# Holding later weights behind the first gathers, and quantising them after the first statistics

## The reference: what is computed

```python
def _L0_tok_ref(inputs, w0, w1):
    x = w0[inputs]
    emb = jnp.einsum('blk,kh->blh', x, w1)
...
def fp4_quant_dequant(x):
    shape = x.shape
    xb = x.reshape(shape[:-1] + (shape[-1] // BLOCK, BLOCK))
    scale = jnp.max(jnp.abs(xb), axis=-1, keepdims=True) / 6.0
    scale = jnp.maximum(scale, jnp.float32(1e-12))
    xn = xb / scale
    idx = jnp.searchsorted(_MID, jnp.abs(xn))
    q = _GRID[idx] * jnp.sign(xn) * scale
    return q.reshape(shape)
...
gate = fp4_linear(x, w_gate)
y = fp4_linear(x, w_up)
h = jax.nn.silu(gate) * y
return fp4_linear(h, w_down)
```

## Time and profile before

| | us |
|---|---|
| median of 3 runs | 788.66 (787.74 to 792.24) |
| the profiled execution, its own time | 790.58 |
| span of the profiled execution, first to last instruction | 788.8 |
| PE busy | 698.7 |
| DVE busy | 600.1 |
| ACT busy | 511.7 |
| POOL busy | 147.8 |

### The profile page before, as it was taken

One profiled execution on the slowest core, in us unless ns is written; L12 is line 12 of the kernel. 1 busy time (PEld: TensorE's weight loads), 2 busy tenths in 40 slices (PEclk: granted clock), 3 DMA queues, 4 the chain that ended last, 5 costly groups with the idle time before them and its releaser, 6 DMA issues.

```text
span 788.8 us, 9882 instructions
## 1 busy us (share of the span) xinstructions
PE 698.7 (89%) x3311; PEld 566.1 (72%) x3311; DVE 600.1 (76%) x1023; ACT 511.7 (65%) x889; POOL 147.8 (19%) x220
## 2 busy tenths in 40 slices
PE   3353699699999999999999999999999999799686
PEld 2231576589688977888688958897789778688574
DVE  0797835987788888788788778888878888863763
ACT  1267488668874887389757886588748974761221
POOL 2042230433023300421022302330131003100000
PEclk9677799899999999999999999999999999899988
DMA  5800000000010000100010001000100000000000
GB/s 133 230 27 25 3 27 0 28 1 27 1 41 14 26 3 14 41 1 27 14 34 8 28 14 27 15 28 0 35 20 1 1 14 15 1 0 14 15 0 27
DMA packets 11956, 19.34 MB, mean 25 GB/s; under 512 B 972, under 2 KB 9346, under 8 KB 11906
## 3 DMA queue, kind: packets, MB, share of 16 engines
q1 hardware_dynamic: 9302, 10.31, 4.5%
q0 software_dynamic: 2560, 8.39, 3.7%
q10 hardware_dynamic: 44, 0.01, 0.0%
HBM read 14.51 MB, written 4.19 MB: 24 GB/s over the span
## 4 chain that ended last, share of the span: by engine, by line
PE 69%; DVE 15%; ACT 7%; issue 6%; DMA 2%; POOL 0%; SPq 0%; DVEq 0%; ACTq 0%; POOLq 0%
PE psB L546 17%; PE psB L573 11%; PE psC L642 11%; PE psC L615 11%; PE psA L537 9%; PE psA L509 3%; PE psC L629 3%; ACT mix L796 2%; DMA kkT<-L_ffn_w_gate 2%; DVE top L352 1%; DVE mix L1082 1%; PE psB L519 1%; PE psA L519 1%; DVE top L949 1%; ACT take L790 1%
## 5 line engine op out<-in xcount | busy, mean ns | idle before, releaser
L546 PE MATMUL psB<-cwv_s,kkT 128*128 128x256 f32 x512 | 113.2, 379 | 0.0
L546 PEld LDWEIGHTS psB<-cwv_s,kkT 128*128 128x128 f32 x512 | 96.6, 190 | 16.0 <-issue 3.7
L642 PE MATMUL psC<-downT,hqT 128*128 128x256 f32 (+1 forms) x384 | 97.0, 398 | 0.0
L429 POOL DMA_INDIRECT rows<-L_tok_w,ids_now x32 | 45.7, 1427 | 266.7 <-PE psA L497 255.1
L615 PE MATMUL psC<-up_hi,xq_hi 128*128 128x352 f32 x256 | 88.3, 345 | 7.4 <-DVE xq_lo L1194 6.8
L642 PEld LDWEIGHTS psC<-downT,hqT 128*128 128x128 f32 (+1 forms) x384 | 70.2, 193 | 26.7 <-issue 19.0
L537 PE MATMUL psA<-mix,kvr_s 128*128 128x512 f32 x192 | 86.8, 596 | 1.5 <-DVE mix L963 1.3
L615 PE MATMUL psC<-up_hi,xq_lo 128*128 128x352 f32 x256 | 84.0, 328 | 0.0
L615 PE MATMUL psC<-up_lo,xq_hi 128*128 128x352 f32 x256 | 83.9, 328 | 0.0
L537 PEld LDWEIGHTS psA<-mix,kvr_s 128*128 128x128 f32 x192 | 35.8, 190 | 41.1 <-issue 38.4
L963 DVE SCALAR_TENSOR_TENSOR mix<-hT,rest,mix 128x512 f32<-128x512 f32 x80 | 54.3, 747 | 10.3 <-ACT mix L744 10.3
(11 more groups left out here) (163 smaller groups left out, 1435.6 us busy)
## 6 DMA issues: line engine op xcount, KB each, us to landing
out<-h SPq DMA_DIRECT2D x16, 256.0 KB, 2.1
mix<-L_attn_cwk SPq DMA_DIRECT2D x1, 1024.0 KB, 15.7
cwv_s<-L_attn_cwv SPq DMA_DIRECT2D x1, 1024.0 KB, 16.0
kkT<-L_ffn_w_gate SPq DMA_DIRECT2D x1, 704.0 KB
kkT<-L_ffn_w_up SPq DMA_DIRECT2D x1, 704.0 KB
hqT<-L_ffn_w_down SPq DMA_DIRECT2D x1, 704.0 KB, 17.9
w_s<-L_tok_w SPq DMA_DIRECT2D x1, 512.0 KB, 4.0
rows<-L_tok_w,ids_now POOLq DMA_INDIRECT x32, 4.1
```

What stands on the lines that cost most here:

```text
L429: pool.indirect_dma_start(rows[:, q, :], None, tok_w0, bass.IndirectOffsetOnAxis(ap=ids_now[:, s, t:t + 1], axis=0)).then_inc(rows_in[q], 16)
L546: mm = nc.tensor.matmul(psB[:, B.slot(name), q * D:(q + 1) * D], lhsT[:, k, (2 * j + q) * P:(2 * j + q + 1) * P], weight[:, k, :], start=( ...
L642: mm = nc.tensor.matmul(psC[:, C.slot(name), 0, q * D:(q + 1) * D], hqT[0:n, q, k, :], downT[0:n, k, :], start=(k == 0), stop=(k == KI - 1))
```

## The change

Two things are changed. SP gets one more wait, on the second pair of gathers, between wr and gate; gate and all the weights behind it are started only then. And three tables are reordered at the start: on DVE w_quant0 goes behind a_stat of chunk 0, and w_quant1 behind a_mix; on ACT w_sq0 goes behind a_emb1, and w_sq1 behind a_part. w_quant2 stands in another place of the table, but at the same place of the resulting order. PE's, POOL's and SP's tables are not touched.

```diff
@@ -70,20 +70,20 @@
         ("c_up0", 2), ("c_cols1", 2), ("a_turn1", 0), ("w_turn1", 1), ("b_cols", 1), ("a_emb1", 0), ("c_up1", 2),
         ("c_turn0", 2), ("b_gate", 1), ("c_up2", 2), ("b_key0", 1), ("a_cols", 0), ("c_turn1", 2), ("b_key1", 1),
         ("c_up3", 2), ("w_turn2", 1), ("b_key2", 1), ("w_turn0", 0), ("a_k", 0), ("b_key3", 1), ("a_v", 0)],
-    "act": [("c_cols1", 1), ("b_part", 0), ("w_sq0", -1), ("c_up1", 1), ("a_emb1", -1), ("b_high", 0),
-        ("w_turn1", 0), ("c_turn0", 1), ("b_gate", 0), ("w_sq1", -1), ("c_sq1", 1), ("a_norm", -1), ("c_up2", 1),
-        ("b_key0", 0), ("c_turn1", 1), ("a_cols", -1), ("c_sq2", 1), ("b_key1", 0), ("a_part", -1), ("w_par", -2),
+    "act": [("c_cols1", 1), ("b_part", 0), ("c_up1", 1), ("a_emb1", -1), ("w_sq0", -1), ("b_high", 0),
+        ("w_turn1", 0), ("c_turn0", 1), ("b_gate", 0), ("c_sq1", 1), ("a_norm", -1), ("c_up2", 1), ("b_key0", 0),
+        ("c_turn1", 1), ("a_cols", -1), ("c_sq2", 1), ("b_key1", 0), ("a_part", -1), ("w_sq1", -1), ("w_par", -2),
         ("c_up3", 1), ("b_key2", 0), ("w_key", -1), ("a_k", -1), ("c_sq3", 1), ("b_key3", 0), ("a_v", -1),
         ("a_wkv1", -1), ("a_wkv2", -1), ("a_r", -1), ("a_wkv3", -1), ("c_turn2", 1), ("w_turn2", 0), ("a_y", -1),
         ("c_turn3", 1), ("c_norm0", 0), ("a_turn0", -2), ("c_sqn0", 0), ("w_turn0", -1), ("c_cols0", 0),
         ("c_norm1", 0), ("a_emb0", -2), ("w_sq2", -1), ("c_sqn1", 0), ("c_up0", 0), ("b_norm", -1), ("a_turn1", -2),
         ("c_sq0", 0), ("b_cols", -1)],
     "dve": [("c_up1", 2), ("b_low", 1), ("c_quant1", 2), ("c_up2", 2), ("w_split1", 1), ("c_quant2", 2),
-        ("a_mix", 0), ("c_up3", 2), ("c_quant3", 2), ("a_wkv1", 0), ("w_key", 0), ("c_down0", 2), ("a_wkv2", 0),
-        ("w_par", -2), ("a_wkv3", 0), ("b_value0", 1), ("c_stat0", 1), ("a_wkv4", 0), ("c_norm0", 1),
+        ("a_mix", 0), ("w_quant1", 0), ("c_up3", 2), ("c_quant3", 2), ("a_wkv1", 0), ("w_key", 0), ("c_down0", 2),
+        ("a_wkv2", 0), ("w_par", -2), ("a_wkv3", 0), ("b_value0", 1), ("c_stat0", 1), ("a_wkv4", 0), ("c_norm0", 1),
         ("b_value1", 1), ("c_stat1", 1), ("c_down1", 2), ("c_split0", 1), ("w_split0", 0), ("b_x1", 0),
-        ("c_norm1", 1), ("w_quant0", -2), ("c_up0", 1), ("c_quant0", 1), ("c_split1", 1), ("w_quant2", 0),
-        ("b_mix", 0), ("a_stat", -1), ("w_quant1", -1)],
+        ("w_quant2", 0), ("c_norm1", 1), ("c_up0", 1), ("c_quant0", 1), ("c_split1", 1), ("b_mix", 0),
+        ("a_stat", -1), ("w_quant0", -1)],
     "pool": [("gather1", 1), ("c_coef0", 3), ("c_coef1", 3), ("b_sum", 2), ("b_coef", 2), ("a_coef", 1),
         ("gather0", 0)],
     "sp": [("c_down1", 3), ("c_down0", 2)],
@@ -381,6 +381,8 @@
                 sp.wait_ge(rows_in[q], 16)
             for k, w in enumerate((wk, wv, wr)):
                 sp.dma_start(kvr_s[:, k], w.rearrange("(k p) d -> p k d", p=P)).then_inc(s_kvr, 16)
+            for q in range(2):
+                sp.wait_ge(rows_in[q], 32)
             for k, w in enumerate((w_gate, w_up)):
                 sp.dma_start(raw_up[:, k * GJ:(k + 1) * GJ, :], w.rearrange("(j p) d -> p j d", p=GP)).then_inc(s_raw[k], 16)
             sp.dma_start(raw_down, w_down.rearrange("(h p) n -> p h n", p=P)).then_inc(s_raw[2], 16)
```

## The result

The changed kernel takes 786.8 us (median of 20 runs, 784.46 to 789.95), the kernel before 789.37 us in as many runs beside it (787.18 to 792.24). The ratio is 0.9969, with a 95% interval of 0.9955 to 0.9983: 2.4 us faster by the ratio, between 1.3 and 3.6 (the two medians lie 2.6 apart).

A forecast was written before the change was run, and what follows sets the result against it. The start was taken as bound by DVE, entered late because of gate's DMA, with the recurrence also waiting on ACT. takev 2.8 us earlier gives 790.58 - 2.8 = 787.8 profiled; the median, 1.92 lower, is 785.9, range 784.0 to 789.2.

The forecast's parts named there:

- Part 1: Second pair of gathers: tile 3 lands at 19.2, between 18.5 and 24.7, instead of 24.7.
- Rival 1: Start-up: gathers stay slow behind wk, wv, wr, or gate does; takev 2.7 or 2.3 us late; chance 0.10.
- Part 2: Embedding job and statistics: e1's matmuls take 3.62 us at full clock, DVE is through a_stat at about 26.1.
- L: Landing time of tile 3, the second pair's slow gather; taken as 19.2.
- Part 3: Gate weight: issued 0.05 us behind tile 3, lands in 5.05 us, hidden under a_stat, costs nothing.
- S: Start of w_quant0 on DVE, the later of a_stat's end and gate's landing; taken as 26.1.
- Part 4: DVE from w_quant0 on: a_wkv1 starts 29.1 us later, at 55.2 against 56.73, 1.5 us earlier.
- Part 5: ACT ahead of the recurrence: first Relu waits only for DVE and starts at 58.2, not 60.96, 2.8 us earlier.
- Rival 2: Start-up: only DVE's part arrives, with v late or e1 at half clock; gain 1.5 to 1.8 us; chance 0.22.
- The sum: Chunk 0's takev moves 2.8 us earlier, carried one for one to the end: median 785.9.
- inner band: Whole kernel: time between 785.2 and 786.6 us around the forecast 785.9, given a chance of 0.50.
- Rival 3: After the start: the gain is swallowed by something at a fixed time further on, 788.7 us; chance 0.08.

The follow-up runs named there:

- order_only: The new orders on DVE and ACT without SP's new wait, against the kernel before: 795.02 us, ratio 1.0073.
- after: First profile of the changed kernel, with the new wait and the new orders, against the kernel before: its profiled execution spans 784.8 us, against 788.8.
- up_behind: The changed kernel, but SP starts up and everything behind it only when gate has landed: 786.55 us in one run.
- after_again: The changed kernel once more, unaltered, as partner on the same chip: 787.44 us, ratio 0.9986 to the kernel before.
- pinned pair: The kernel before and the changed kernel, each with 92 and 22 throwaway transposes in two idle gaps of PE: 786.81 and 784.27 us.
- wait_only: SP's new wait with the orders of before, against the kernel before: 791.24 us, ratio 1.0021.
- warm_out: The changed kernel with 64 throwaway transposes on PE ahead of chunk 0's output projection: 785.99 us, ratio 0.9961 to the kernel before.
- before_steady: The kernel before with 92 throwaway transposes ahead of chunk 0's projection and 22 ahead of the last tile's transposes: 786.81 us, ratio 0.9970.

## Why the prediction was right, step by step

**Part 1, right.** Tile 3 at 18.7, near the fast bound of 18.5; 19.2 was taken. order_only shows the other side: with only the wait missing it is 9.35 us again. Rival 1, that wk, wv and wr are to blame, is refuted: in after they travelled beside the gathers, and tile 3 took 4.39 us where the first tile had taken 4.26. One reading in this part was off without harm: the 24.67 that DVE shows is the landing of gate, and only PE and the earlier trace rows tell that tile 3 was as late.

**Part 2, right.** e1 took 3.62, and a_stat began at 23.88, 5.2 behind tile 3; it was through at about 25.6, L + 6.9.

**Part 3, wrong in size.** Gate was given 5.05 us and hidden; it took 7.64, and DVE waited 0.80 for it. The term that failed is the line through two transfers of 128 partitions, applied to one of 88. It cost little because tile 3 was 0.5 earlier than assumed: S became 26.41 instead of 26.1. Two errors of opposite sign, which is luck: with gate in 5.05 us S would have been 25.6. The other value on record, the estimate of 6.8 us by the rule of the Trainium skill ("DMA: Bandwidth & Descriptors", same section as above), was the better one, and up_behind measured 6.8 for gate alone.

**Part 4, right.** S + 29.1 = 55.5; the scan began at 55.45, without waiting for k.

**Part 5, right, but without margin.** The first Relu was forecast at S + 32.1 = 58.5 and came at 58.50. The forecast had it released by DVE, with vT1 copied 0.4 earlier; in the profile vT's copy ended at 58.47, level with `gain`. v and r took 9.19 us, not the 7.10 of full clock, and v alone 5.8 (52.08 to 57.87), not the 5.2 that were taken. In after_again the copy began at 56.89, and the Relu of 58.01 waited 0.52 for DVE, as forecast. So the clock at v costs nothing until v is later than DVE, and there it stood on the edge. Rival 2 was near: in up_behind, with S = 25.60, v was the later one and took 0.5 us of the lead.

**The sum.** takev came 2.44 us earlier in the first profile, where 2.8 was forecast, and 2.8 on the mean of four profiles each; at the end it is 2.5 with two clocks pinned and 2.4 in 20 runs (1.3 to 3.6). The time itself, 786.8, lies 0.9 above the forecast 785.9, 0.2 outside its inner band of 785.2 to 786.6 and next to rival 2's 787.0. Of these 0.9 us 0.7 come from the base: before has a median of 789.37 in 20 runs, not the 788.66 of the first three. The interval of the gain holds rival 2's 1.5 to 1.8 us as well, so it is the rows that speak for the forecast (scan at 55.45, first Relu at 58.50), not the total. What the working had not seen is that "one for one to the end" holds in a single pair of runs only when the clock is the same at two places: the projection right behind (5.1 to 6.6 us in the unfilled kernels) and the last 24 matmuls (5.9 or about 8). Rival 3, the lead swallowed later, seemed to show in the first pair (2.44 to 1.80), but the pinned pair keeps its lead to within 0.1 us. after_again, at 1.1 us (0 to 2.3), shows how much of the gain the clock can hide.

## What to carry to other kernels

A transfer that the first computation needs should not share its start with megabytes that are needed 10 us later: here one wait on the issuing engine brought it in 6 us earlier. The wait paid only together with an order of work that uses what comes early and covers what now comes late; check both halves alone, as each of them here made the kernel slower. Look also at what an order hides: the old one let the clock at k reach the result, the new one doesn't. When a change is worth 0.3%, compare the same place in both traces along the whole run before believing the difference of two spans, and where equal work differs in length, fill PE's idle time ahead of it, so that its clock is the same in both kernels.

## What the runs showed of the hardware

- **Gathers beside a loaded queue.** The second pair's last gather took 9.3 to 10.3 us in the five profiles in which SP had gate and all the weights behind it started, and 3.9 to 4.4 us in the nine with wk, wv and wr alone, though the profile lists the two kinds of transfer on different queues.
- **88 partitions.** 704 KB over 88 partitions took 6.8 us alone (up_behind, one profile), where a line through 256 and 512 KB over 128 partitions (2.6 and 4.0 us) gives 5.05.
- **The clock after idling.** The same 16 matmuls of the projection took 5.11, 5.50, 5.60, 5.70, 5.90, 6.05, 6.58 and 6.62 us in eight profiles after the same 12 us of idling, and 3.69 behind the filling; the granted clock read 0.50 at their start in each. The last 24 matmuls took 5.93 us in four and 7.57 to 8.07 in four of the eight profiles in which the gap ahead of their transposes was 3.06 us (3.05 in one). In three more (wait_only, warm_out, up_behind) this gap was only 1.67 to 1.88 us, and they took 5.93 each time, as in all three with the filling.
- **Throwaway work pays.** Keeping PE busy in these two gaps alone made the kernel before 0.3% faster (before_steady: 0.9970, 0.9953 to 0.9987), as much as the change under study.
